# Rows ahead of key weights, and two token lists moved into the first expert

## The reference

```
h = weight[ids]                                     # gather of rows
h = h + attention(layernorm(h))                     # 8 heads of 128, rotary, causal
x = layernorm(h)                                    # 4096 tokens
scores = softmax(x @ Wr)                            # 8 experts
G, idx = top_k(scores.T, 1024)                      # 1024 tokens for each expert
y_e = gelu(x[idx_e] @ W1_e + b1_e) @ W2_e + b2_e    # 256 -> 1024 -> 256
out = h;  out[idx_e] += G_e * y_e
```

## Time and profile before

| what | value |
|---|---|
| median of 3 runs | 1184.82 us (1183.53 to 1185.37) |
| the profiled execution | 1191.39 us |
| its span, first to last instruction | 1189.6 us |
| mean granted TensorE clock | 0.996 of full |
| TensorE busy | 1143.3 us, 96% |
| VectorE, ScalarE, GpSimd busy | 825.0, 721.2, 821.1 us |

### The profile page before, as it was taken

How to read it: one execution, slowest core, us unless ns; L and a number is a source line. 1 busy time by engine, 2 the same in 40 slices (tenths; PEclk the granted TensorE clock), 3 DMA queues, 4 the chain that set the end, 5 groups by cost and what they waited for, 6 DMA issues and landing times. The chain is left out here.

```text
span 1189.6 us, 20415 instructions
## 1 busy us (share of the span) xinstructions
PE 1143.3 (96%) x7120; PEld 997.1 (84%) x7120; DVE 825.0 (69%) x1994; ACT 721.2 (61%) x1537; POOL 821.1 (69%) x921
## 2 busy tenths in 40 slices
PE   7899999999999999999999998779999999999997
PEld 4788888888888888888888885358999999999996
DVE  5998887887887887887888867864455554554433
ACT  4667677686686676676676765315465555555642
POOL 4798897897897898887987854052474484664425
PEclk9999999999999999999999999999999999999999
DMA  5000100100100100200101003322362452523213
GB/s 199 10 10 1 45 28 2 45 28 1 45 28 1 55 18 2 71 2 29 43 2 36 19 1 114 110 69 75 61 139 33 111 127 31 129 51 94 32 23 36
DMA packets 43030, 58.13 MB, mean 49 GB/s; under 512 B 8944, under 2 KB 34992, under 8 KB 42800
## 3 DMA queue, kind: packets, MB, share of 16 engines
q0 software_dynamic: 13824, 21.24, 10.0%
q1 hardware_dynamic: 29104, 35.58, 8.8%
HBM read 35.71 MB, written 16.91 MB: 44 GB/s over the span
## 5 line engine op out<-in xcount | busy, mean ns | idle before, releaser
L1462 DVE TENSOR_TENSOR hT_lo<-hid,hT_hi 128x512 fp32r<-128x512 f32 x124 | 86.2, 695 | 170.7 <-ACT hT_hi L1638 155.6
L312 ACT ACTIVATE prob<-prob,row_min 128x512 f32<-128x512 f32 (+3 forms) x256 | 141.8, 557 | 103.0 <-DVE row_min L539 103.0
L1635 ACT ACTIVATE hid<-up,b_e 128x512 f32<-128x512 f32 x128 | 88.1, 688 | 156.9 <-PE up L1790 137.0
L227 POOL TENSOR_SCALAR prob<-prob,row_inv 128x512 f32<-128x512 f32 (+3 forms) x256 | 134.8, 541 | 12.3 <-DVE row_inv L552 10.3
L1176 POOL DMA_INDIRECT x<-routed_rows,tokens x64 | 81.4, 1272 | 76.7 <-DVE tokens L1456 38.8
L235 POOL TENSOR_TENSOR q_sin<-q_sin,rope_t 128x512 f32<-128x512 f32 x64 | 82.7, 1292 | 73.7 <-ACT q_sin L336 73.7
L444 DVE TENSOR_TENSOR pT_lo<-bank,pT_hi 128x384 fp32r<-128x384 f32 (+1 forms) x192 | 110.2, 594 | 15.4 <-ACT pT_hi L288 14.2
L1187 POOL TENSOR_SCALAR y<-y,gate 128x256 f32<-128x256 f32 x60 | 32.2, 548 | 127.1 <-issue 126.4
L1196 POOL DMA_INDIRECT out<-y,tokens x60 | 98.6, 1643 | 16.2 <-issue 13.9
L799 PE MATMUL bank<-ident,prob 128*128 128x128 f32 x640 | 102.1, 274 | 5.7 <-POOL prob L227 5.0
L288 ACT ACTIVATE pT_hi<-bank 128x384 fp32r<-128x384 f32 (+1 forms) x192 | 96.5, 519 | 13.7 <-PE bank L799 13.3
(11 more groups left out here) (337 smaller groups left out, 3895.3 us busy)
## 6 DMA issues: line engine op xcount, KB each, us to landing
raw<-in_w SPq DMA_DIRECT2D x16, 1024.0 KB
emb_res<-emb SPq DMA_DIRECT2D x8, 512.0 KB, 3.8
out<-h SPq DMA_DIRECT2D x8, 512.0 KB, 2.9
routed_rows<-x SPq DMA_DIRECT2D x8, 512.0 KB, 3.0
x<-in_wq SPq DMA_DIRECT2D x2, 512.0 KB, 6.4
x<-in_wk SPq DMA_DIRECT2D x2, 512.0 KB, 6.4
x<-in_wv SPq DMA_DIRECT2D x2, 512.0 KB, 4.1
x<-in_wo SPq DMA_DIRECT2D x1, 1024.0 KB, 10.1
```

The source lines that it names most:

```text
L227: nc.gpsimd.tensor_scalar(pr, pr, row_inv[:, h % 2, k:k + 1], 1.0, ALU.mult, ALU.mult).then_inc(s["norm_done"], 1)
L312: nc.scalar.activation(pr, pr, ACT.Exp, bias=row_min[:, h % 2, k:k + 1], scale=-1.0, accum_out=row_sum[:, h % 2, k:k + 1]).then_inc(s["exp ...
L1462: nc.vector.tensor_tensor(out, in_, hi.bitcast(F32), ALU.subtract)\
L1635: nc.scalar.activation(hid[:, t % 2, :], up_ps[t % 2][:], ACT.Gelu, bias=bias)
```

## The change

At the start, SP asks for the key weights only after the rows have landed, and for the rotation table after the value weights' a half. ScalarE's high part of the key weights moves behind the mask, the `xT` copies move ahead of the value a high part. VectorE's query low part moves ahead of the statistics. Ten filling products follow attention. Lists 1 and 2 are both made in expert 0: list 1 at steps 0, 3 and 4 and list 2 at steps 11, 13 and 14. There are more filling products before list 0 (20 for 16), after it (25 for 18) and before each block of the first transposes (4 for 2).

```diff
@@ SP
-            load("k", "a")
-            sp.dma_start(rope_t[:], a["rope"][:, :, :]).then_inc(s["rope_in"], 16)
             for tb in range(TB):
                 sp.wait_ge(s[f"first_emb{tb}"], 16)
+            load("k", "a")
             load("v", "a")
+            sp.dma_start(rope_t[:], a["rope"][:, :, :]).then_inc(s["rope_in"], 16)
@@ ScalarE
             split_high("q", "a")
-            split_high("k", "a")
             act.wait_ge(s["mask_in"], 16)
...
+            split_high("k", "a")
+            xt(0)
             split_high("v", "a")
-            xt(0)
             split_high("v", "b")
@@ VectorE
+            split_low("q", "a", 1)
             for tb in range(TB):
...
-                if tb == 1:
-                    split_low("q", "a", 1)
@@ TensorE, end of attention
             batches(pe, body)
+            warm(10)
@@ VectorE, before and in expert 0
             dve.wait_ge(s["placed"], 2)
-            one_hots(1)
-            write_list(1, 1)
...
+                    if e == 0 and t == 0:
+                        one_hots(1)
+                    if e == 0 and t == 4:
+                        write_list(1, 1)
                     if more2:
-                        if t == 0:
+                        if t == (11 if e == 0 else 0):
                             one_hots(e + 2)
-                        if t == 5:
+                        if t == (14 if e == 0 else 5):
                             write_list(e + 2, i)
@@ TensorE, before and in expert 0
                 for c in range(TB):
-                    warm(2)
+                    warm(4)
...
-            warm(16)
+            warm(20)
             pe.wait_ge(s["hot_b0"], 1)
             write_list(0)
-            warm(18)
-            write_list(1)
+            warm(25)
             first_turn()
...
-                    if more2 and t == (4 if e == 0 else 2):
+                    if e == 0 and t == 3:
+                        write_list(1)
+                    if more2 and t == (13 if e == 0 else 2):
                         write_list(e + 2)
```

## The result

The changed kernel takes 1188.37 us (median of 9 runs, 1187.28 to 1189.28), the kernel before, in the same comparison, 1185.11 (9 runs, 1183.53 to 1186.05): ratio 1.0028, 95% interval 1.0019 to 1.0037. It is 3.3 us slower. Forecast were 1188.6 us and a sum of 3.8. The profiled execution of the changed kernel took 1187.93 us (span 1186.1).

The account below looks back on a forecast made before the run. TensorE, without idle time in the expert phase, was taken as the bound. Start 0, end of attention 0, turn 0.7, lists 1.0 and stall 2.1 sum to 3.8 us, added to the 1184.82 median: 1188.6, range 1182.0 to 1190.8.

Parts of the forecast that it names:

- Start, 0: First 25 us: earlier means offset by late key weights and value low part; value products at 20.45, bounds -1.2 to +1.6.
- the forecast's own signs of being wrong: No step-12 wait, ScalarE copying xT within 1 us of transposes in a faster run, or value products a microsecond early.
- the rival of -1.2: Start gains 1.2 us if the value low part is not last: 1187.4, within the main case's range; no separate chance.
- packet-by-packet rule: Start: DMA engines alternate between queues, so gathers gain little from moving the key load; start would cost 0.5, sum 4.3.
- End of attention, 0: Ten filling products after TensorE's last output product cost nothing beside evacuation and store; 1.7 us without that cover.
- Turn, +0.7: Search to expert 0: more filling makes the fourth block's transposes start at 789.1 instead of 788.38; bounds 0 and 0.7.
- Lists, +1.0: Expert 0 makes two lists instead of one: 32 more products on TensorE, which has no idle time, +1.0 us.
- the stall, +2.1: Expert 0, step 12: TensorE waits for VectorE's xT low part behind list 2's one-hots, +2.1 us; bounds 0 and 2.2.
- GpSimd's moves, 0: Gathers 1 and 2 and the adding of expert 0's first half move later; GpSimd catches up within two experts, 0.
- The rival of the late signals: Turn: moving list 1 away removes unexplained waits and slow clock worth 6.2 us, so 2.4 faster, 1182.4; chance 0.20.
- Clock lost at the start: TensorE's new gaps at the start cost its clock, some 1.6 us: sum 5.4, 1190.2; chance 0.11.

Follow-up runs that it names:

- experiment 9: Kernel before, gather 1's eight issues spread out, each waiting for one more low half of the hidden values: 1185.90 us, ratio 1.0006 to the kernel before.
- experiment 11: Changed kernel with list 2's one-hots at step 9 and two filling products a block (22 ahead of them), on a later chip: 1184.21 us, ratio 0.9993 to before.
- experiment 1: Kernel before, unchanged, one more profiled run on another chip: 1192.36 us.
- experiment 5: Changed kernel as it is, on another chip than the first comparison: 1191.48 us, ratio 0.9965 to the kernel before.
- experiment 3: Changed kernel with the three start edits put back, so the turn alone: 1191.15 us, ratio 0.9966 to the kernel before.
- experiment 4: Changed kernel with list 2's one-hots at step 9 of expert 0 instead of 11: 1189.61 us, ratio 0.9957 to the kernel before.
- experiment 12: Experiment 11 with each gather for the expert after next issued behind the first half's addition: 1185.16 us, ratio 1.0003 to the kernel before.
- experiment 2: Kernel before with the start's edits alone (SP's order, ScalarE's order, query low part ahead of statistics): 1194.05 us, ratio 0.9995 to the kernel before.
- experiment 7: Changed kernel with two filling products a block instead of four, and 22 instead of 25 ahead: 1187.86 us, ratio 0.9940 to the kernel before.
- experiment 8: Changed kernel with list 2's one-hots at step 9, two filling products a block and 22 ahead: 1186.24 us, ratio 0.9922 to the kernel before.
- experiment 6: Kernel before with gather 1 held back until VectorE's third low half of the hidden values: 1196.19 us, ratio 1.0013 to the kernel before.
- experiment 10: Kernel before with four filling products ahead of each block instead of two: 1186.56 us, ratio 1.0011 to the kernel before.

## Why it came out as it did

A common clock makes the kernels comparable: the start of gather 0's first issue on GpSimd, the tenth and the twentieth Gelu into hid behind it (one per step: step 9 of expert 0 and step 3 of expert 1), and the end of the span. No profile shows the kernel before without late signals. I take experiment 9 in its place, whose turn and lists are those of before; it differs in when gather 1 is issued, and its median is 0.7 us above the kernel before. ScalarE's two rows, of experiment 9, the changed kernel and experiment 11:

```profile
820.25 0.69 ACT L1637 ACTIVATE hid<-up,b_e 128x512 f32<-128x512 f32 x1 [1.57 <-PE up L1792]
...
851.47 0.69 ACT L1637 ACTIVATE hid<-up,b_e 128x512 f32<-128x512 f32 x1 [2.79 <-PE up L1792]
```

```profile
818.59 0.69 ACT L1637 ACTIVATE hid<-up,b_e 128x512 f32<-128x512 f32 x1 [1.56 <-PE up L1792]
...
853.20 0.69 ACT L1637 ACTIVATE hid<-up,b_e 128x512 f32<-128x512 f32 x1 [2.79 <-PE up L1792]
```

```profile
817.10 0.69 ACT L1637 ACTIVATE hid<-up,b_e 128x512 f32<-128x512 f32 x1 [1.57 <-PE up L1792]
...
849.49 0.69 ACT L1637 ACTIVATE hid<-up,b_e 128x512 f32<-128x512 f32 x1 [2.79 <-PE up L1792]
```

Gather 0's first issue is at 783.49, 781.06 and 780.74 in the three; the spans are 1184.4, 1186.1 and 1182.4. The same readings of three more profiles stand below them.

| us | gather 0 to tenth | tenth to twentieth | twentieth to end |
|---|---|---|---|
| before (experiment 9) | 36.76 | 31.22 | 332.9 |
| changed | 37.53 | 34.61 | 332.9 |
| one-hots at 9, two fillings (11) | 36.36 | 32.39 | 332.9 |
| before, profile of the earlier trace rows | 44.34 | 31.22 | 333.0 |
| before, experiment 1 | 45.89 | 31.21 | 333.0 |
| changed, experiment 5 | 38.00 | 34.61 | 334.8 |

Point by point:

*Start, 0.* In this profile the value products moved by 0.10, but two steps of the sum were off and cancelled. The gathers were not in at 10.16: the third issue took 1.99 us, and 0.95 in experiment 3 with the old start, so the fourth was issued at 8.34 instead of 7.31. It then landed 2.8 us later, as forecast from the turn's gather. And GpSimd's value low part took 2.41 us, not 3.24, which gave back what the late key weights had cost. The 3.24 of the earlier trace rows was read where VectorE's key low part ran beside it,

```profile
15.69 1.22 DVE L444 TENSOR_TENSOR wk_lo<-x,wk_hi 128x1024 fp32r<-128x1024 f32 x1
```

and with the new start that one is over before the value low part begins. It takes 3.24 to 3.27 us in all six profiles with the old start and 2.41 or 2.42 in all eight with the new one.

The long third issue, however, is not always there. It is in three of the eight profiles with the new start (this one, experiments 4 and 12: 1.87 to 1.99 us), where VectorE's query low part began 0.05 to 0.17 us before it. In the other five (2, 5, 7, 8 and 11) VectorE began at most 0.04 before it, or after it, and the issue took 0.95. There the last mean ends at 10.7, as forecast, and the value products begin at 19.35 to 19.48. Experiment 5, the same kernel, shows it in three rows:

```profile
6.05 0.95 POOL L200 DMA_INDIRECT emb<-in_emb,ids  x1 [0.30 <-issue]
...
10.14 0.38 SPq L147 DMA_DIRECT2D x<-in_wk  x1
...
19.41 0.50 PE L707 MATMUL bank<-wv_hi,xT_hi 128*128 128x512 f32 x1
```

That is a microsecond early, one of the forecast's own signs of being wrong: the value low part took 0.83 us less than the sum has and began 0.2 earlier (16.94 for 17.15), and the rival of -1.2 is nearer to these five. Gather 0's first issue at the turn comes at 780.0 to 781.5 in the eight profiles (mean 780.7) and at 780.5 to 783.5 in the six with the old start (mean 781.8), in kernels that differ in the filling too. A gain of about 1 us is likely, but the timed runs do not show it: experiment 2's interval holds 0 as well.

By the packet-by-packet rule of the Trainium skill (DMA: Bandwidth & Descriptors, Queues, rings and completion order), moving the key load away should hardly help the gathers. The trace disagrees again for the first one, issued at 3.33 in both kernels and used at 7.13 instead of 9.79.

*End of attention, 0.* Nothing speaks against it: gather 0 starts at 781.06, before 781.09, and at 781.07 in experiment 3, which has the ten fillings and the old start. The five profiles with the old start and without the fillings scatter from 780.5 to 783.5, so half a microsecond would not be seen.

*Turn, +0.7.* Right: 37.53 - 36.76 = 0.77. The fourth block's transposes start 7.98 us after gather 0 (789.04 - 781.06) instead of 7.23 (790.72 - 783.49 in experiment 9).

*Lists, +1.0, and the stall, +2.1.* Right: between tenth and twentieth the changed kernel has 34.61 - 31.22 = 3.39 more, and with the one-hots at step 9 (experiment 11) it has 1.17 more. So list 2's products in a later step cost 1.2 and the stall 2.2; the wait in the profile is 2.00.

*GpSimd's moves, 0.* Right: 332.9 in both.

The terms as measured make 0.8 + 3.4 = 4.2, the runs 3.3, with an interval of 2.2 to 4.4. With a gain of about 1 us at the start the sum would be 3.2. That the forecast of 3.8 came so near is in part luck: it has the stall and the lists a little short and the start at nothing.

*The rival of the late signals* was priced at 6.2 and given 0.20, with the remark that the timed runs may not have them. It was right, but not everywhere. The profile of before has 44.34 - 36.76 = 7.6 us of them, the timed runs of the first comparison, by their time, none, those on two other chips about 9 to 10 (1195.27 and 1194.47 against 1185.18; 45.89 - 36.76 = 9.1 in experiment 1, 11.6 in experiment 2). Where they are there, the change takes them from the turn and finds one of 1.9 us beside gather 3 (334.8 - 332.9): 4.2 - 9.1 + 1.9 = -3.0, and -3.0 was measured between experiment 5 and its kernel before. The agreement to a tenth is luck, since the 9.1 is one profile of another chip and the next has 11.6; the sign and the size are what this shows. What makes a signal late on one chip and not on another, in rows of indirect gathers that are issued alike, stays open, and so does whether the rows, list 1 beside them, or both are needed. Spreading the issues, or moving them behind the additions, was tried only where nothing was to be cured.

*Clock lost at the start.* Not seen as an effect of the change: the granted clock over the first 40 us is 0.96 in the changed kernel's profile (0.91 over the first 20), but it was 1.00 in experiments 2, 5 and 11 with the same start, and it also fell with the old one: 0.91 in experiments 3 and 6, 0.96 in experiment 10.

Of the fixes, the one-hots at step 9 and two fillings a block together bring the changed kernel to 0.9993 (0.9984 to 1.0002) on a chip without late signals, which is no difference from the kernel before, and to 0.9922 on one with them. It had the lowest median on both chips where it ran.

## What to carry to other kernels

Before a small operation is moved into a loop whose limiting engine has no idle time, look at what is queued behind it on its own engine: the one-hots cost nothing as work and 2.2 us as the thing that an in-order queue put ahead of the copy that empties TensorE's PSUM bank; two steps earlier they cost nothing. Filling products between gathered blocks are free only while the last of them ends before the last gather lands: two a block did, four made it 0.8 us late. A duration is read with what ran beside it: the value low part's 3.24 us was 2.41 at another place. And when a profile shows waits that no work explains, compare its time with the timed runs and repeat the kernel before on another chip: the sign of a change of 0.3% depended on it.

## What the runs showed of the hardware

- TensorE's signals reached ScalarE and VectorE 2.4 to 5.7 us late while GpSimd issued rows of eight or sixteen indirect gathers, on two of the three chips of the experiments, at 9 to 10 us in all for the kernel before, and on the third not at all. On the same two chips other rows of eight had no late signal beside them.
- The third indirect gather's issue on GpSimd took 0.95 us in eleven profiles, also where VectorE's subtraction of 1.23 to 1.29 us ran beside it but began at most 0.04 us before it, and 1.87 to 1.99 in three, where the subtraction had begun 0.05 to 0.17 us before.
- The same subtraction of 128 x 1024 on GpSimd took 3.24 to 3.27 us in the six profiles where its first 1 us lay beside VectorE's key low part (15.93 and 15.69 in the kernel before), and 2.41 or 2.42 in the eight where that one was over and only VectorE's low part of xT ran beside it.
- After one stall of 2.0 us TensorE's granted clock fell to 0.66 over 5 us in one profile (experiment 3) and stayed at 1.00 in two others (the changed kernel, experiment 5).
